# Quantised feed-forward of a gated eight-stage block: where the last pass gets its products, who turns integers to floats, and when gated values are loaded

## The reference, cut to what matters

```python
def act_qdq(x):
    qmax = 2.0 ** (ACT_BITS - 1) - 1.0
    scale = jnp.maximum(jnp.max(jnp.abs(x)) / qmax, 1e-12)
    return jnp.clip(jnp.round(x / scale), -qmax - 1.0, qmax) * scale
...
x = act_qdq(x)
up = act_qdq(x @ lpbq_dequant(w_up).T)
gate = act_qdq(x @ lpbq_dequant(w_gate).T)
sig = fixed_qdq_u16(jax.nn.sigmoid(gate))
gate = act_qdq(gate * sig)
o = act_qdq(gate * up)
return o @ lpbq_dequant(w_down).T
...
x = x + jnp.tanh(g_ffn[3]) * _L3_ffn_ref(_layernorm(x, axis=-1), L3_ffn_w_gate, L3_ffn_w_up, L3_ffn_w_down)
```

## Time and profile before

| | us |
|---|---|
| median of 3 runs | 2269.8 |
| lowest, highest | 2269.4, 2273.78 |
| the profiled execution, its own time | 2268.44 |
| its span in the profile | 2266.7 |
| mean granted TensorE clock over the span | 0.944 of full speed |
| PE busy over the span | 1969.5 (87%) |
| DVE busy | 1731.4 (76%) |
| ACT busy | 1219.1 (54%) |

### The profile page before, as it was taken

One profiled execution on the slowest core, in us unless ns is written; L12 is line 12 of the kernel. 1 busy time (PEld: TensorE's weight loads), 2 busy tenths in 40 slices (PEclk: granted clock), 3 DMA queues, 4 the chain that ended last, 5 costly groups with the idle time before them and its releaser, 6 DMA issues. The chain is left out here.

```text
span 2266.7 us, 48312 instructions
## 1 busy us (share of the span) xinstructions
PE 1969.5 (87%) x18173; PEld 1512.4 (67%) x18173; DVE 1731.4 (76%) x4753; ACT 1219.1 (54%) x2340; POOL 262.7 (12%) x553
## 2 busy tenths in 40 slices
PE   3999999999987999999989896999999994699517
PEld 3787888878767987777757574677777773344217
DVE  2888888888867978999957796667666588787886
ACT  2555555555552217888856463445444355209647
POOL 0111111111101102111111142000000022100000
PEclk9999999999997999999989897999999997799759
DMA  6122221112214541111100011221122110003532
GB/s 184 47 51 50 51 50 47 48 48 51 50 28 188 226 188 33 32 30 33 30 4 1 10 57 47 89 99 76 75 100 88 47 48 20 1 0 123 189 133 75
DMA packets 123592, 155.71 MB, mean 69 GB/s; under 512 B 47562, under 2 KB 104291, under 8 KB 119267
## 3 DMA queue, kind: packets, MB, share of 16 engines
q1 hardware_dynamic: 117368, 149.92, 20.4%
q10 hardware_dynamic: 5994, 2.70, 0.4%
HBM read 110.11 MB, written 25.69 MB: 60 GB/s over the span
## 5 line engine op out<-in xcount | busy, mean ns | idle before, releaser
L1717 DVE TENSOR_TENSOR arena<-arena 128x512 f32<-128x512 f32 (+1 forms) x256 | 170.8, 685 | 68.9 <-ACT arena L1755 64.7
L1755 ACT ACTIVATE arena<-banks,b1c 128x512 f32<-128x512 f32 x192 | 131.7, 687 | 170.4 <-PE banks L1630 170.2
L1640 PEld LDWEIGHTS banks<-w2a,arena 128*128 128x128 f32 x1024 | 124.1, 192 | 28.7 <-issue 28.7
L885 PE MATMUL banks<-we,arena 128*128 128x128 f32 x1024 | 130.2, 282 | 3.2
L885 PEld LDWEIGHTS banks<-we,arena 128*128 128x128 f32 x1024 | 121.1, 194 | 10.1 <-DVE arena L949 9.8
L498 PE MATMUL banks<-arena,wk 128*128 128x128 f32 x1024 | 126.8, 278 | 1.1 <-DVE arena L606 1.1
L539 PE MATMUL banks<-wv,arena 128*128 128x512 f32 x256 | 125.1, 611 | 2.6 <-ACT arena L652 2.6
L1640 PE MATMUL banks<-w2a,arena 128*128 128x128 f32 x1024 | 124.7, 275 | 0.0
L498 PEld LDWEIGHTS banks<-arena,wk 128*128 128x128 f32 x1024 | 121.0, 194 | 1.7 <-DVE arena L606 1.5
L1630 PE MATMUL banks<-arena,w1s 128*128 128x512 f32 x256 | 122.0, 611 | 0.0
L633 ACT ACTIVATE arena<-banks 128x512 f32<-128x512 f32 x64 | 38.2, 597 | 143.6 <-PE banks L490 143.6
(11 more groups left out here) (271 smaller groups left out, 5110.2 us busy)
## 6 DMA issues: line engine op xcount, KB each, us to landing
arena<-coef_scratch SPq DMA_DIRECT2D x32, 2048.0 KB, 7.1
arena<-arena SPq DMA_DIRECT2D x256, 64.0 KB, 2.0
gated_scratch<-arena SPq DMA_DIRECT2D x16, 768.0 KB, 3.2
arena<-gated_scratch SPq DMA_DIRECT2D x16, 768.0 KB, 4.3
arena<-z1T_scratch SPq DMA_DIRECT2D x128, 64.0 KB, 2.3
arena<-ctxT_scratch SPq DMA_DIRECT2D x32, 256.0 KB, 2.8
arena<-in_ctx SPq DMA_DIRECT2D x64, 64.0 KB, 2.0
z1T_scratch<-arena SPq DMA_DIRECT2D x64, 64.0 KB, 1.7
```

The source lines that it names most:

```text
L885: mm = pe.matmul(ps[:, OUT + g.par, j * D:(j + 1) * D], xs[g.par][:, n, j * P:(j + 1) * P], k.we0[:, n, :], start=n == 0, stop=n == EXPERT ...
L1640: mm = pe.matmul(ps[:, OUT + g.par, j * D:(j + 1) * D], hT[g.par][:, c, j * P:(j + 1) * P], w, start=c == 0, stop=c == CHUNKS2 - 1)
L1717: dve.tensor_tensor(hT[g.par][rows, c, :], hT[g.par][rows, c, :], wide_coef[g.par][rows, e, :], ALU.mult).then_inc(s["scaled"].sem, 1)
L1755: act.activation(hT[g.par][:, c, :], ps[:, HID + c % NHID, :], ACT.Gelu, bias=k.b1c[:, c:c + 1])\
```

## The change

Three things are changed in `quantised3`, and the memory plan with them:

1. The products of the third pass get 16 places in place of two. Eight lie where `xdT` and part of the first buffers of the second pass lay, seven over `upq` (the place of group 8+n covers the `upq` of groups 2n and 2n+1, which have been used by then), one in `gin[0]`. The last pass no longer computes them again; `oprod` and the helper `product` are gone. In return `gq2` has two buffers in place of sixteen, so ACT waits for the product of two groups before, and the same two int16 buffers serve as `oq` in the last pass.
2. In the last pass ACT only rounds the product (L2088 of the kernel before), into two buffers in place of one. DVE turns the integers to floats with `tensor_copy`, ahead of the update of `x` of the group before.
3. `gin[0]` now has a place that nothing of the second pass uses. Its load waits for its own group's store alone. The load into `gin[1]`, which lies over buffers of the second pass, still waits for all stores and all maxima; later ones wait for their buffer as before.

```diff
-    xhs = k.take(T * P).rearrange("p (g n) -> p g n", g=G)
-    mark = k.taken
-    gq2 = k.arena[:, mark - 2 * T * P:mark - 2 * T * P + G * W // 2].bitcast(I16).rearrange("p (g n) -> p g n", g=G)
...
-    gin, prod = [k.take(W) for _ in range(2)], [k.take(W) for _ in range(2)]
-    k.taken = mark - 2 * T * P + G * W // 2
-    oprod, oq, of = k.take(W), half(W), [k.take(W) for _ in range(2)]
+    gin = [k.take(W)]
+
+    k.taken = turned
+    prod = [k.take(W) for _ in range(8)] + [k.arena[:, n * W:(n + 1) * W] for n in range(G - 9)] + [gin[0]]
+    gin.append(k.take(W))
+    gq2 = [half(W) for _ in range(2)]
+    of, oq = [k.arena[:, (G - 9) * W:(G - 8) * W], gin[1]], gq2
...
         steps(sp, G, 0, 0, store)
-        gs_stored.wait_all(sp, G)
-        sp.wait_ge(*s["gsmax"].all(G))
 
         def load(at):
             if g := at(0):
-                if g.has(2):
+                sp.wait_ge(*gs_stored(g))
+                if not g.has(1):
+                    sp.wait_ge(*s["gs"](g))
+                elif not g.has(2):
+                    gs_stored.wait_all(sp, G)
+                    sp.wait_ge(*s["gsmax"].all(G))
+                else:
                     sp.wait_ge(*s["gq2"](g.back(2)))
                 sp.dma_start(gin[g.par], gs_dram[g.idx]).then_inc(gs_loaded.at(g), 16)
...
         def third(at):
             if g := at(1):
                 dve.wait_ge(*s["gq2"](g))
-                if g.has(2):
-                    dve.wait_ge(*s["omax"](g.back(2)))
-                product(g, prod[g.par], s["prod"])
+                if G // 2 <= g.idx < G - 1:
+                    dve.wait_ge(*s["prod"](Tile(2 * (g.idx - G // 2) + 1, 1)))
+                dve.scalar_tensor_tensor(out=prod[g.idx], in0=gq2[g.par], scalar=sprod[:, :], in1=upq[:, g.idx, :],
+                                         op0=ALU.mult, op1=ALU.mult).then_inc(s["prod"].sem, 1)
...
         def last(at):
-            if g := at(2):
-                if g.has(1):
-                    dve.wait_ge(*s["oq"](g.back(1)))
-                product(g, oprod, s["oprod"])
+            if g := at(1):
+                dve.wait_ge(*s["oq"](g))
+                if g.has(2):
+                    dve.wait_ge(*s["y_psum"](g.back(2)))
+                dve.tensor_copy(of[g.par], oq[g.par]).then_inc(s["of"].sem, 1)
             if g := at(0):
                 dve.wait_ge(*s["y_psum"](g))
                 x = k.x[:, bass.ds(g.idx * GROUP, GROUP), :].rearrange("p j n -> p (j n)")
                 dve.scalar_tensor_tensor(out=x, in0=ps[:, g.par, :], scalar=down[:, :], in1=x, op0=ALU.mult,
                                          op1=ALU.add).then_inc(f["x_updated"].sem, GROUP)
-        steps(dve, G, 2, 0, last)
+        steps(dve, G, 1, 0, last)
...
         def third(at):
             if g := at(0):
                 act.wait_ge(*gs_loaded(g))
-                k.hold(act)
-                act.activation(gq2[:, g.idx, :], gin[g.par], ACT.Copy, scale=inv["gs"][:, :])\
+                if g.has(2):
+                    act.wait_ge(*s["prod"](g.back(2)))
+                act.activation(gq2[g.par], gin[g.par], ACT.Copy, scale=inv["gs"][:, :])\
                     .then_inc(s["gq2"].sem, 1)
...
         def last(at):
             if g := at(0):
-                act.wait_ge(*s["oq"](g))
                 if g.has(2):
-                    act.wait_ge(*s["y_psum"](g.back(2)))
-                act.activation(of[g.par], oq, ACT.Copy).then_inc(s["of"].sem, 1)
-            if g := at(1):
-                act.wait_ge(*s["oprod"](g))
-                if g.has(1):
-                    act.wait_ge(*s["of"](g.back(1)))
-                act.activation(oq, oprod, ACT.Copy, scale=inv["o"][:, :]).then_inc(s["oq"].sem, 1)
-        steps(act, G, 1, 0, last)
+                    act.wait_ge(*s["of"](g.back(2)))
+                act.activation(oq[g.par], prod[g.idx], ACT.Copy, scale=inv["o"][:, :]).then_inc(s["oq"].sem, 1)
+        steps(act, G, 0, 0, last)
```

More of the change, by code:

```diff
@@ L1790, in quantised3 @@
     upq = half(G * W).rearrange("p (g n) -> p g n", g=G)
+    turned = k.taken
     xdT = k.take(T * P).rearrange("p (g n) -> p g n", g=G)
+    mark = k.taken
     xhs = k.take(T * P).rearrange("p (g n) -> p g n", g=G)
-    mark = k.taken
-    gq2 = k.arena[:, mark - 2 * T * P:mark - 2 * T * P + G * W // 2].bitcast(I16).rearrange("p (g n) -> p g n", g=G)
-    k.taken = mark - T * P
+    k.taken = mark
     gq, sig, sigq = [half(W) for _ in range(2)], [k.take(W) for _ in range(2)], k.take(W // 2).bitcast(U16)
     gs = [k.take(W) for _ in range(2)]
-    k.taken = max(mark - 2 * T * P + G * W // 2, mark - T * P)
-    gin, prod = [k.take(W) for _ in range(2)], [k.take(W) for _ in range(2)]
-    k.taken = mark - 2 * T * P + G * W // 2
-    oprod, oq, of = k.take(W), half(W), [k.take(W) for _ in range(2)]
+    gin = [k.take(W)]
[4 more added lines that the diff above has]
+    of, oq = [k.arena[:, (G - 9) * W:(G - 8) * W], gin[1]], gq2
     sb = k.sb
@@ L1818, in quantised3 @@
         shift=2, xhs=GROUP, xmax=1, xq=1, xd=1, t_psum=1, xdT=1, p_psum=2 * CHUNKS3, pmax=2 * CHUNKS3, c_psum=2 * CHUNKS3, upq=CHUNKS3,
-        gq=CHUNKS3, sig=1, sigq=1, gs=1, gsmax=1, gq2=1, prod=1, omax=1, oprod=1, oq=1, of=1, y_psum=1))
+        gq=CHUNKS3, sig=1, sigq=1, gs=1, gsmax=1, gq2=1, prod=1, omax=1, oq=1, of=1, y_psum=1))
     SCALES = ("x", "ug", "gs", "o")
@@ L1994, in vector @@
         dve.wait_ge(final, 1)
-        def product(g, out, signal):
-            dve.scalar_tensor_tensor(out=out, in0=gq2[:, g.idx, :], scalar=sprod[:, :], in1=upq[:, g.idx, :],
-                                     op0=ALU.mult, op1=ALU.mult).then_inc(signal.sem, 1)
         def third(at):
@@ L2009, in third @@
                 k.hold(dve)
-                dve.tensor_reduce(omax[:, bass.ds(g.idx, 1)], prod[g.par], AX.X, ALU.max, apply_absolute_value=True)\
+                dve.tensor_reduce(omax[:, bass.ds(g.idx, 1)], prod[g.idx], AX.X, ALU.max, apply_absolute_value=True)\
                     .then_inc(s["omax"].sem, 1)
```

## The result

The changed kernel took 2250.36 us, median of 4 runs (2245.5 to 2253.36), the kernel before in the same rounds 2270.2. The ratio is 0.9917, its 95% interval 0.99 to 0.9935: 19.8 us faster, where 13.6 were forecast.

What follows compares the result with a forecast made beforehand. No engine full; bound by the last pass's alternation of product and rounding (3.46 us a group) and both passes' starts. Gains 11.65 + 2.0 = 13.65 us: 2268.44 to 2254.8, 1.4 more for the median, 2256.2; range 2252.8 to 2261.2.

Steps and rivals of the forecast that it cites:

- the mechanism of the last pass: Last pass: product and rounding stop alternating (3.46 us a group) and PE sets the pace; gain 11.65 us.
- From there DVE sets the pace as before, 3.59 a group: Third pass after product 2: DVE keeps 3.59 us a group, so only the start gains.
- DVE's own work: 1.82 us for a product, 1.75 for a maximum, 0.03 between: Third pass: the 3.59 us between maxima was taken as DVE's work alone.
- The clock: Last pass start: PE at the 1.2 GHz level as before; first group 5.50 us, 0.3 extra for the second.
- the prediction's 5.8: Last pass before the change: full clock level said to return 5.8 us after the first matmul.
- the 1.1 that the range allowed: Last pass: 2.3 us less time at half speed would give 1.1 us more gain.
- PE's pace: Last pass: PE never waits and takes 2.73 us a group, the middle of 2.79 and 2.67; upper bound 2.95.
- weight loads alone set PE's pace: Rival, last pass: 2.67 us or less a group, 0.9 us less, about 2255.3; 15%.
- The 2.6 us that the range allows for PE's pace: Last pass: downward part of the range from 2256.2, for a faster PE.
- The early load: Third pass start: load 0 issued 3.3 us earlier, landing at 2135.3, product 2 sooner; gain 2.0 us.
- a delay that the prediction named: Third pass: load 0 might delay store 15 and so load 1 onward; 1 us allowed in the range.
- The start of the last pass: From `inv_o` to the first matmul: conversion 0.96 us, first matmul at 2201.94, 2.6 us sooner than before.

Runs made afterwards that it cites:

- third_product_buffer: Kernel before with a third product buffer in the third pass, so product g waits for the maximum of g-3; 2268.07 us, ratio 0.9992.
- wait_for_maximum: Changed kernel with the wait of product g for the maximum of g-2 put back; 2258.7 us, ratio 0.9939.
- late_first_load: Changed kernel with the third pass's first load waiting again for all stores and all maxima; 2256.04 us, ratio 0.9931.
- last_pass_alone: Changed kernel with the wait for the maximum of g-2 and the late first load both put back; 2258.32 us, ratio 0.9955.
- act_turns_to_float: Changed kernel with ACT instead of DVE turning the integers to floats in the last pass; 2256.42 us, ratio 0.9945.
- pe_warm_longer: Changed kernel with idle PE matmuls: 26 and 8 around the scale of x, 8 ahead of up and gate's, 58 and 20 around o's; 2248.54 us, ratio 0.9906.

## Why the prediction was wrong, point by point

The direction held, and so did the mechanism of the last pass; that of the third did not, and the forecast gain was too small by 6.2 us in the medians. In the traces the two passes gained 18.1, the forecast had 13.65.

- **The step that failed** is "From there DVE sets the pace as before, 3.59 a group", and ahead of it the reading of 3.59 as "DVE's own work: 1.82 us for a product, 1.75 for a maximum, 0.03 between". The sum fitted and was wrong twice. The records of consecutive DVE instructions overlap by about 0.08, so the work alone is 3.39. The other 0.20 was a wait: in DVE's order the maximum of g-2 stands right ahead of product g, so `omax(g.back(2))` waited for DVE's own last instruction to complete. The diff removes that line, and I had costed its removal at nothing without saying so. It is worth 2.5 us in the pass, from either side (third_product_buffer, wait_for_maximum). The rows that the prediction shows do not name it, since DVE's instructions have no idle time before them there; the chain of a few microseconds does, as `DVEq L2005`.
- **The clock** was taken to come back as in the trace of before, 6.1 us after the first matmul (the prediction's 5.8 is misread, which leaves its sum as it is). It took 3.2. The first group, with that, was 1.0 us shorter and the second 0.3, a little more than the 1.1 that the range allowed. This part of the gain is luck as far as the runs show: late_first_load and last_pass_alone, with the same last pass, had 5.6 for the first group again. But all three traces of the changed kernel itself had 4.6 or 4.7 and none with the old last pass did, so whether the earlier start makes it likelier stays open.
- **PE's pace** was 2.68, not 2.73: 0.75 us over 15 groups. The rival "weight loads alone set PE's pace" had 2.67, from rows, and its number was right; that it is the weight loads which set the pace, no run here shows. The Trainium skill, "TensorE: Matmul & The Clock Gate", section "LDWEIGHTS (loading the stationary operand)", gives 107 ns a load, which would be 2.56; the trace has 40.2 / 15 / 24 = 0.1117, 4.7% above it. The 2.6 us that the range allows for PE's pace come from that figure of the page; by the rows it would have been 0.9, and that was enough.
- **The early load**: 1.5 us (late_first_load) against 2.0. Load 0 landed 5.93 us after the last gated value was ready (2130.48 to 2136.41), where the prediction had 5.5. And the last store took longer with the load right behind it and held back load 1 by 0.9 us, a delay that the prediction named and left out of its sum. The third product was released by ACT's rounding of group 2, on the path over load 0; the one over load 1 was some 0.2 us shorter. From there on the loop of load, rounding, load never held up DVE.
- **The start of the last pass**: 2.7 us from `inv_o` to the first matmul, the conversion 0.96, both as worked out.
- **The median.** I set the gain against 2269.8. Over all rounds the kernel before has a median of 2269.9 in 54 runs and the changed one of 2252.4 in 16, 17.5 apart, which fits the 17.9 to 18.1 us of the passes. The first four runs of the changed kernel were 2 us on the low side. Chance of that size lies in the stages ahead: `inv_gs` fell between 2131.4 and 2135.5 in three traces of the same kernel. The 2252.4 of all runs is still below the range, by 0.4.

So of the 4.4 us by which the passes beat the forecast, 2.5 is the wait (0.5 less for the load), 1.3 the clock and 0.75 the pace, 4.1 in all; the rest is not placed. With the wait in the sum the forecast would have been 2253.7. A range for a kernel whose runs differ by 10 us should have been wider as well.

## What to carry to other kernels

When a wait is removed, ask which instruction signals it and where that one stands in the waiter's own order: a wait for the instruction just ahead on the same engine costs its completion, 0.2 us each time on DVE here, and no idle time in the profile stands for it. To see it, take starts and not durations: if start to start is more than with the same two instructions elsewhere, something stands between. Then ask for the chain of those few microseconds: a `DVEq` entry with the line of the wait names it. With two buffers and an order of "next product, then maximum" the reuse wait always hits the last instruction; a third buffer takes it off.

## What the runs showed of the hardware that was not expected

- Records of consecutive instructions overlap. DVE: a product after a maximum starts 1.66 us after it, though the maximum lasts 1.75. ACT: four roundings of 1.575 us took 5.97, which is 1.47 from start to start. Sums of durations are too long by about 0.1 an instruction here.
- A DVE instruction that waits for the one ahead starts 0.20 us later than one that doesn't (1.86 against 1.66). The Trainium skill, "VectorE: DVE Perf Modes", section "The DRAIN you can't avoid", has it that a semaphore after each of eight `tensor_copy` operations costs nothing extra; the runs here say otherwise for a wait between a maximum and a product, and they decide for this pair.
- After some 60 us in which PE did next to nothing, the granted clock returned from the 1.2 GHz level between 3.0 us (act_turns_to_float) and 6.1 us (last_pass_alone, before) after the first matmul, with PE busy all the while. The first group took between 4.5 and 5.6 us with that, for the same instructions. After idle matmuls that kept the clock at 2.4 GHz it was 3.0 or 3.1.
- A store of 768 KB with a load of 768 KB issued right behind it took 4.02 us to land (2129.56 to 2133.58, the chain of pe_warm_longer), and 3.23 alone (before, late_first_load).
